# The end of a two-layer graph kernel: buffers of their own for the last normalisation, and another order of its loads and stores

## Chip, cores and metric

One NeuronCore of a Trainium2 chip runs the whole program. The metric is the device time of one execution in microseconds. One execution was recorded with the profiler; its times below count from the first instruction (the span's start).

## What is computed

x has 2048 rows of 512. A layer norm and a quantised graph layer give x1; then comes the layer that the end of the kernel works on:

```python
S = adj + I;  R = S / row_sums(S);  Xf = Xa = X = relu(layernorm(x1));  Z = 0
for s in range(2):
    A  = top_p_softmax(Xa @ W1 @ W2 @ (Xa @ W3).T)       # rows, P_TOP = 0.9
    Xf = R @ Xf
    Xa = A @ Xa
    Z  = Z + (Xf @ U1[s] + Xa @ U2[s])
Y = X + Z
out = x1 + (Y - mean(Y)) * rsqrt(var(Y) + 1e-5) * gamma + beta
```

## The kernel before

The 2048 rows are 16 tiles of 128 (T = 16), in four groups of four (G = 4, NG = 4). The second layer has two steps, s = 0 and 1. In step 1 each tile needs three things: its row of the diffusion R, added on GpSimd and written to the HBM tensor z1_d (`r_sum` line 651, `r_store` 396); its attention row, made on VectorE (`search`, `settle`), which leaves E's slot of the tile in two half-precision parts and signals `s_kept`; and the product of the attention row with the operand in VR.

**One tile on the way to the product.** `e_turned` (line 469) transposes the slot with four DMA transposes, one for each 512 columns, into the single buffer EC. Each waits until TensorE has used the same part for the tile before (`s_a`). `terms_product` (931) multiplies; 48 matmuls make a tile. ScalarE scales the result by `rden` (1260), which exists once VectorE has finished all four tiles of the group (1806). GpSimd adds the z that SyncE loaded from z1_d into ZT (`z_in` 429, sum in 698). ZT is one buffer, so `z_in(t)` waits for the sum of tile t - 1. Slots of E alternate: groups 0 and 2 use slots 0 to 3, groups 1 and 3 slots 4 to 7.

**The order around a group** is fixed by `step_order` (265): for each group `group_start`, which takes the rows of R that fall to it (one in group 0, four in groups 1, 2 and 3 of step 1), then `pairs` with its four tiles. All DMAs stand in SyncE's one queue, in program order; a wait there holds up everything behind it. A row of R needs three loads (`at_hi_in`, `at_lo_in`, `ad_in`, lines 384 to 394) and one store.

**The end.** Tiles 0 to 11 are normalised in three batches of four, tiles 12 to 15 one by one (`normed` 1833, `batch`, `end`, 1851 to 1867). VectorE takes batch 0, batch 1, tile 12, batch 2, tiles 13, 14, 15. The inverse root of each comes from GpSimd (`root` 682), whose order in the last group is: root of batch 0, sum of tile 12, roots of batch 1, tile 12 and batch 2, sum of tile 13, its root, sum and root of tile 14, of tile 15. A batch needs y from z1_d and x from x1_d, 1 MB each (`fin_in` 442), in E's slots 0 and 1 or 2 and 3: batch 2 uses the buffers of batch 0 and so waits for its store (`s_out`). All these loads are issued in `pairs` of the last group (491 to 498), ahead of the transposes of tile 13, and batch 2's at tile 13 (517). Tiles 12 to 15 lie in turn in UO and XF, so tile 14 waits for the store of tile 12 (1258); their x rows (`end_in` 457) go to WS, VectorE's scratch.

Of the kernel before, what the change touches and what calls it, by code (L numbers as in the profile page):

```python
# [8 lines left out]
P = 128  # L9
N, D, DA = 2048, 512, 64  # L10
T = N // P
KC = D // P
G = 4
# [85 lines left out]
def build(nc, x, adjT, scal, w, W1T, W2, W3, U10, U11, U20, U21, gamma, beta, out):  # L99
    ctx = ExitStack()  # L100
    with ctx:
# [79 lines left out]
        fin_y = [E[:, 2 * h, :].rearrange("p (t d) -> p t d", t=G) for h in range(2)]  # L181
        fin_x = [E[:, 2 * h + 1, :].rearrange("p (t d) -> p t d", t=G) for h in range(2)]
# [5 lines left out]
        gam, ends = WF, (UO, XF)  # L188
        end_x = WS[:, :].rearrange("p (t d) -> p t d", t=G)
# [59 lines left out]
        s_finx, s_finy, s_end = ([sem(f"{n}{h}") for h in range(2)] for n in ("s_finx", "s_finy", "s_end"))  # L249
        s_endx = sem("s_endx")  # L250
# [48 lines left out]
        def _(sp):  # L299
# [142 lines left out]
            def fin_in(b):  # L442

                rows = slice(G * b, G * b + G)
                if b >= 2:
                    sp.wait_ge(s_out, 16 * (b - 1))
                sp.dma_start(fin_x[b % 2], x1_d[rows].rearrange("t p d -> p t d")).then_inc(s_finx[b % 2], 16)
                sp.wait_ge(s_yout, 16 * (G * b + G) + OPEN)
                sp.dma_start(fin_y[b % 2], z1_d[rows].rearrange("t p d -> p t d")).then_inc(s_finy[b % 2], 16)

            def fin_out(b, nth):
                sp.wait_ge(s_res, nth)
                if b:
                    sp.wait_ge(s_out, 16 * b)
                sp.dma_start(out[G * b:G * b + G].rearrange("t p d -> p t d"), fin_y[b % 2]).then_inc(s_out, 16)

            def end_in():
                sp.wait_ge(s_kept, 2 * T)
                sp.dma_start(end_x, x1_d[T - G:T].rearrange("t p d -> p t d")).then_inc(s_endx, 16)

            def end_out(t, nth):
                sp.wait_ge(s_res, nth)
                sp.dma_start(out[t], ends[t % 2][:, :]).then_inc(s_end[t % 2], 16)
# [14 lines left out]
            def group_start(s, g):  # L478
                if s == 0 and g:
                    stores(G * g - 1)  # L480
                rows = diffusion(s, g)
                for rs, t in rows[:-1]:
                    r_done(rs, t, t % 2)
                for c in range(NC):
                    e_turned(g * G + s * T, g * G % (2 * G), c)
                for rs, t in rows[-1:]:
                    r_done(rs, t, t % 2)

            def pairs(s, g):
                last = s == 1 and g == NG - 1  # L490
                if last:
                    sp.wait_ge(s_wl, T)
                    sp.wait_ge(s_gb, 16)
                    sp.dma_start(gam[:, :], gamma.partition_broadcast(P)).then_inc(s_gb, 16)
                    for c in range(NC):
                        sp.wait_ge(s_et[c], 16 * (T + G * (NG - 1)))
                    fin_in(0)
                    fin_in(1)
                for i in range(G):
                    t = g * G + i  # L500
                    following = (t + 1 + s * T, (t + 1) % (2 * G))
                    if s:
                        z_in(t)
                    if i < G - 1:
                        for c in range(NC - 1):
                            e_turned(*following, c)
                    if s == 0 and i:
                        stores(t - 1)
                    if i < G - 1:
                        e_turned(*following, NC - 1)  # L510
                    if s and not last:
                        y_store(t)
                    if last and i == 0:
# [35 lines left out]
            end_out(T - G + 2, 6)  # L549
            end_out(T - G + 3, 7)  # L550
            sp.wait_ge(s_rout, 16 * T + OPEN)
            sp.wait_ge(s_out, 16 * BATCHES)
            for h in range(2):
                sp.wait_ge(s_end[h], 16 * (G // 2))
# [3 lines left out]
        def _(pool):  # L558
# [127 lines left out]
            def pairs(s, g):  # L686
                for i in range(G):
# [7 lines left out]
                    y = ends[t % 2] if g == NG - 1 else UO  # L695
# [350 lines left out]
        def _(act):  # L1046
# [200 lines left out]
            def a_out(s, g, t, slot, bank):  # L1247
# [72 lines left out]
        def _(dve):  # L1320
# [530 lines left out]
            def batch(b, nth):  # L1851
                dve.wait_ge(s_finx[b % 2], 16 * (b // 2) + 16)
                dve.wait_ge(s_finy[b % 2], 16 * (b // 2) + 16)
                normed([(G * b + t, fin_y[b % 2][:, t, :], fin_x[b % 2][:, t, :]) for t in range(G)], nth)

            def end(t, nth):
                dve.wait_ge(s_y, t + 1 + OPEN)
                normed([(t, ends[t % 2][:, :], end_x[:, t - (T - G), :])], nth)
# [37 lines left out]
```

## Time and profile before

| | |
|---|---|
| three runs, median (lowest to highest) | 1296.33 us (1292.09 to 1300.24) |
| profiled execution, its own time | 1295.24 us |
| its span | 1293.3 us |
| TensorE busy | 1119.5 us, 87% |
| VectorE busy | 1035.7 us, 80% |
| ScalarE, GpSimd busy | 439.4 us, 281.2 us |
| mean granted TensorE clock | 0.953 |
| moved by DMA | 170.62 MB, mean 132 GB/s |

The busy shares are averages over the whole span. The end has limits of its own: in the last 25 us of the trace TensorE, VectorE and the DMA engines all have holes, so the chain of waits and the timelines of that stretch say more than the table. A bracket at the end of a row of a timeline gives the idle time of that engine before it, and what ended it.

### The profile page before, as it was taken

What the parts mean: (1) busy time and instruction counts of PE and PEld (TensorE: products, weight loads), DVE (VectorE), ACT (ScalarE), POOL (GpSimd) and SP (SyncE); (2) the same over time, 40 slices, a digit from 0 to 9 for tenths busy, and PEclk for the clock granted to TensorE, in tenths of its full rate; (3) what the DMA queues carried; (4) which work ended last, traced back from release to release, by engine and by line L of the source; (5) the groups of instructions that cost most, each with busy time, mean ns of one, the idle gap of its engine ahead of it and who ended that gap; (6) DMA issues with size and microseconds to landing.
All of it is one profiled execution on the core that took longest, in us unless ns stands there. A gap on an engine that the chain in (4) does not pass through costs nothing.

```text
span 1293.3 us, 16644 instructions
## 1 busy us (share of the span) xinstructions
PE 1119.5 (87%) x5402; PEld 518.1 (40%) x5402; DVE 1035.7 (80%) x2202; ACT 439.4 (34%) x836; POOL 281.2 (22%) x252
## 2 busy tenths in 40 slices
PE   0567999998999799799997999898999799789764
PEld 0223445454434344344443444343444344334321
DVE  7987777773599998899698006998997999999965
ACT  2544344444633033533432237540241251100000
POOL 6133333333122200101112010421111021011012
PEclk9888999999999899899998999898999899899887
DMA  7126466453334542341732513236844552743595
GB/s 244 65 69 220 166 205 209 168 199 118 95 117 153 143 89 43 90 82 42 147 82 66 96 51 130 90 117 243 193 91 136 134 115 90 187 114 107 148 266 156
DMA packets 190115, 170.62 MB, mean 132 GB/s; under 512 B 144656, under 2 KB 144656, under 8 KB 185936
## 3 DMA queue, kind: packets, MB, share of 16 engines
q1 hardware_dynamic: 190032, 169.66, 46.7%
q8 instruction: 34, 0.56, 0.2%
q14 instruction: 49, 0.40, 0.1%
HBM read 87.31 MB, written 48.76 MB: 105 GB/s over the span
## 4 chain that ended last, share of the span: by engine, by line
DVE 34%; PE 27%; issue 20%; POOL 7%; DMA 5%; ACT 5%; SPq 1%; POOLq 1%; DVEq 1%; ACTq 0%
PE RB L937 5%; DVE WS L1490 5%; DVE cand L1708 4%; PE UB L775 4%; PE AB L937 4%; DVE E L1721 3%; PE XB L775 3%; DVE WS L1705 3%; DVE WS L1713 3%; PE RB L939 3%; DVE g L1570 2%; PE AB L939 2%; DMA AD<-xu_d 2%; DVE E L1461 2%; DVE E L1720 2%
## 5 line engine op out<-in xcount | busy, mean ns | idle before, releaser
L1570 DVE TENSOR_REDUCE g<-E 128x1 f32<-128x2048 f32 x32 | 73.0, 2281 | 100.3 <-ACT E L1160 100.0
L1490 DVE SCALAR_TENSOR_TENSOR WS<-E,g 128x2048 bf16<-128x2048 f32 x48 | 119.6, 2535 | 0.4
L655 POOL TENSOR_TENSOR RT<-RT,AD 128x512 f32<-128x512 f32 x32 | 56.5, 1765 | 289.3 <-ACT RT L1220 289.2
L1708 DVE MAX8 cand<-WS 128x8 f32<-128x128 f32 x512 | 102.1, 276 | 1.1
L937 PE MATMUL AB<-VR,turns 128*128 128x512 f16 x256 | 66.3, 406 | 27.7 <-DMA turns<-E 27.7
L1713 DVE SCALAR_TENSOR_TENSOR WS<-E,g 128x2048 f32<-128x2048 f32 x33 | 80.9, 2450 | 0.9
L937 PE MATMUL RB<-VR,turns 128*128 128x512 f16 x256 | 64.2, 396 | 19.5 <-DMA turns<-E 19.5
L1721 DVE SCALAR_TENSOR_TENSOR E<-WS,E 128x2048 f16<-128x2048 f32 x32 | 79.1, 2472 | 1.1
L937 PE MATMUL RB<-XR,turns 128*128 128x512 f16 x256 | 63.8, 394 | 17.9 <-DMA turns<-E 17.9
L1197 ACT ACTIVATE E<-E,nmx 128x2048 f32<-128x2048 f32 x32 | 63.7, 1993 | 42.9 <-DVE nmx L1571 42.9
L672 POOL TENSOR_TENSOR XHL<-WF,XHL 128x512 f16<-128x512 f32 x16 | 22.1, 1383 | 250.0 <-ACT XHL L1245 250.0
L1705 DVE SCALAR_TENSOR_TENSOR WS<-E,g 128x2048 f32<-128x2048 f32 x32 | 75.5, 2360 | 1.1
L758 PE MATMUL AB<-E,turns 128*128 128x512 f16 x256 | 61.6, 397 | 8.9 <-DVE E L1391 5.9
L937 PE MATMUL AB<-XR,turns 128*128 128x512 f16 x256 | 62.3, 387 | 8.0 <-DMA turns<-E 8.0
L1407 DVE TENSOR_REDUCE E<-E (+1 forms) x16 | 59.2, 3703 | 3.1 <-issue 2.6
L899 PE MATMUL AB<-VR,turns 128*128 128x512 f16 x256 | 61.5, 379 | 0.0
L765 PE MATMUL AB<-E,turns 128*128 128x512 f16 x256 | 61.3, 384 | 0.0
L899 PE MATMUL AB<-XR,turns 128*128 128x512 f16 x256 | 56.7, 379 | 2.8 <-POOL XR L618 2.8
L899 PE MATMUL RB<-VR,AH 128*128 128x512 f16 x256 | 56.9, 379 | 0.0
L698 POOL TENSOR_TENSOR UO<-UO,Khl 128x512 f32<-128x512 f32 x14 | 25.3, 1804 | 145.0 <-ACT UO L1260 140.8
L899 PE MATMUL RB<-XR,AH 128*128 128x512 f16 x256 | 56.6, 379 | 0.1
L1412 DVE SCALAR_TENSOR_TENSOR turns<-E,turns (+1 forms) x16 | 38.7, 2420 | 21.0 <-ACT turns L1071 21.0
(316 smaller groups left out, 2210.0 us busy)
## 6 DMA issues: line engine op xcount, KB each, us to landing
turns<-adj_parts SPq DMA_DIRECT2D x48, 512.0 KB, 3.8
E<-adjT SPq DMA_DIRECT2D x16, 1024.0 KB, 7.6
adj_parts<-turns SPq DMA_DIRECT2D x16, 1024.0 KB, 5.2
AH<-adj_parts SPq DMA_DIRECT2D x16, 512.0 KB, 4.1
z_d<-UO SPq DMA_DIRECT2D x28, 256.0 KB, 2.3
XR<-x SPq DMA_DIRECT2D x4, 1024.0 KB, 11.8
WS<-U SPq DMA_DIRECT2D x4, 1024.0 KB, 7.5
x_d<-WF SPq DMA_DIRECT2D x16, 256.0 KB, 2.0
```

Source lines behind the costliest of these rows:

```text
L758: mm(AB[:, :], turns[:, h, 0, j, :], sup[:, j, :], start=(j == 0), stop=False)
L775: i = mm(dst, a(k), b(k), start=(first and n == 0), stop=(last and n == 3 * KC - 1))
L899: i = mm(bank[:, :], at_hi[odd][:, j, :], vs[:, j, k % 2, :], start=(k == 0), stop=False)
L937: mm(bank[:, :], EC[:, c, 0, b, :], xs[:, c * KC + b, y_, :], start=(c + b + y_ == 0), stop=False)
L939: i = mm(bank[:, :], EC[:, c, 1, b, :], xs[:, c * KC + b, 0, :], start=False, stop=(c == NC - 1 and b == KC - 1))
L1197: a(E[:, slot, :], E[:, slot, :], ACT.Exp, bias=nmx[:, slot:slot + 1], accum_out=tot[:, slot:slot + 1]).then_inc(s_exp, 1)
L1490: return v.scalar_tensor_tensor(junk[t % 2], e, g4[:, k, t:t + 1], e, op, ALU.mult, accum_out=g4[:, F_, t:t + 1])
L1570: ct(v.tensor_reduce(row(A2)[:, t:t + 1], E[:, slot, :], AX.X, ALU.max))
L1705: ct(v.scalar_tensor_tensor(WS[:, :], E[:, slot, :], g4[:, U, t:t + 1], E[:, slot, :], ALU.is_lt, ALU.mult, accum_out=g4[:, F_, t:t + 1]))
L1708: i = v.max(cand[:, t, 8 * c:8 * c + 8], WS[:, c * PART:(c + 1) * PART])
L1713: return v.scalar_tensor_tensor(WS[:, :], E[:, slot, :], g4[:, k, t:t + 1], E[:, slot, :], ALU.is_ge, ALU.mult, accum_out=g4[:, DEN, t:t + 1])
L1721: v.scalar_tensor_tensor(lo, kept, SE, hi, ALU.mult, ALU.subtract).then_inc(s_kept, 1)
```

## The change

The three batches get buffers that nothing else uses at that time: y in slots 0, 1 and 2 of E, x in UW, UV (weights of step 0) and slot 3 of E. Tiles 12 to 15 get one buffer each (UO, XF, RT, AD), and their x rows lie in XR instead of WS. The loads of x for batches 0 and 1 and of gamma are issued at the start of group 2 of step 1; y of batches 0 and 1 and x of batch 2 at the start of group 3, y of batch 2 after the first row of R there. In the last group the load of z for tile t + 1 stands behind the transposes of tile t + 1, the load of the x rows for the end behind those of tile 13, and all stores of results stand behind the last transposes and the last load of z. GpSimd's and VectorE's orders are unchanged.

```diff
-        fin_y = [E[:, 2 * h, :].rearrange("p (t d) -> p t d", t=G) for h in range(2)]
-        fin_x = [E[:, 2 * h + 1, :].rearrange("p (t d) -> p t d", t=G) for h in range(2)]
+        fin_y = [E[:, b, :] for b in range(NG - 1)]
+        fin_x = [u[:, :, :, :].rearrange("p k h d -> p (k h d)").bitcast(F32) for u in (UW, UV)] + [E[:, NG - 1, :]]
+        fin_y, fin_x = ([u.rearrange("p (t d) -> p t d", t=G) for u in us] for us in (fin_y, fin_x))
+        end_x = XR[:, 0:G, :, :].rearrange("p t h d -> p t (h d)").bitcast(F32)
...
-        gam, ends = WF, (UO, XF)
-        end_x = WS[:, :].rearrange("p (t d) -> p t d", t=G)
+        gam, ends = WF, (UO, XF, RT, AD)
...
-            def fin_in(b):
-
-                rows = slice(G * b, G * b + G)
-                if b >= 2:
-                    sp.wait_ge(s_out, 16 * (b - 1))
-                sp.dma_start(fin_x[b % 2], x1_d[rows].rearrange("t p d -> p t d")).then_inc(s_finx[b % 2], 16)
+            def fin_x_in(b):
+                sp.dma_start(fin_x[b], x1_d[G * b:G * b + G].rearrange("t p d -> p t d")).then_inc(s_finx[b], 16)
+
+            def fin_y_in(b):
                 sp.wait_ge(s_yout, 16 * (G * b + G) + OPEN)
-                sp.dma_start(fin_y[b % 2], z1_d[rows].rearrange("t p d -> p t d")).then_inc(s_finy[b % 2], 16)
+                sp.dma_start(fin_y[b], z1_d[G * b:G * b + G].rearrange("t p d -> p t d")).then_inc(s_finy[b], 16)
...
             def group_start(s, g):
                 if s == 0 and g:
                     stores(G * g - 1)
+                if s == 1 and g == 2:
+                    sp.wait_ge(s_wl, T)
+                    fin_x_in(0)
+                    fin_x_in(1)
+                    sp.wait_ge(s_gb, 16)
+                    sp.dma_start(gam[:, :], gamma.partition_broadcast(P)).then_inc(s_gb, 16)
+                if s == 1 and g == NG - 1:
+                    for c in range(NC):
+                        sp.wait_ge(s_et[c], 16 * (T + G * (NG - 1)))
+                    fin_y_in(0)
+                    fin_y_in(1)
+                    fin_x_in(2)
                 rows = diffusion(s, g)
-                for rs, t in rows[:-1]:
+                for j, (rs, t) in enumerate(rows[:-1]):
                     r_done(rs, t, t % 2)
+                    if s == 1 and g == NG - 1 and j == 0:
+                        fin_y_in(2)
...
             def pairs(s, g):
                 last = s == 1 and g == NG - 1
-                if last:
-                    sp.wait_ge(s_wl, T)
-                    sp.wait_ge(s_gb, 16)
-                    sp.dma_start(gam[:, :], gamma.partition_broadcast(P)).then_inc(s_gb, 16)
-                    for c in range(NC):
-                        sp.wait_ge(s_et[c], 16 * (T + G * (NG - 1)))
-                    fin_in(0)
-                    fin_in(1)
                 for i in range(G):
...
-                    if s:
+                    if s and (i == 0 or not last):
                         z_in(t)
...
                     if last and i == 0:
+                        sp.wait_ge(s_r, 2 * T)
                         end_in()
-                        fin_out(0, 1)
-                    if last and i == 1:
-                        fin_in(2)
-                        fin_out(1, 2)
-                    if last and i == 2:
-                        end_out(T - G, 3)
-                        fin_out(2, 4)
-                    if last and i == 3:
-                        end_out(T - G + 1, 5)
+                    if last and i < G - 1:
+                        z_in(t + 1)
+                if last:
+                    fin_out(0, 1)
+                    fin_out(1, 2)
+                    end_out(T - G, 3)
+                    fin_out(2, 4)
+                    for k in range(1, G):
+                        end_out(T - G + k, 4 + k)
...
                     if t >= T - G + 2:
-                        act.wait_ge(s_end[t % 2], 16)
-                    y = ends[t % 2] if t >= T - G else UO
+                        act.wait_ge(s_rout, 16 * T + OPEN)
+                    y = ends[t % G] if t >= T - G else UO
```

## Rows read from the trace of the kernel before

**Rows 1.** Chain of waits, 1228 to 1294: start us, duration us, what.
```profile
1230.86 0.07 DVE rden L1806
...
1249.85 0.99 POOL rstd L684
...
1265.69 1.45 POOL rstd L684
1267.14 1.58 POOL XF L698
...
1269.17 3.46 DMA turns<-E
...
1272.77 3.57 PE RB L937 x8
...
1284.69 0.88 PE RB L939 x4
...
1289.98 0.75 DVE XF L1848
```

**Rows 2.** VectorE's timeline, the end: start us, duration us, instruction.
```profile
1230.97 2.47 DVE L1838 BATCH_NORM_STATS2 st<-E 128x6 f32<-128x512 f32 x4
...
1236.73 3.62 DVE L1848 SCALAR_TENSOR_TENSOR E<-E,rstd 128x512 f32<-128x512 f32 x4
...
1246.03 2.74 DVE L1848 SCALAR_TENSOR_TENSOR E<-E,rstd 128x512 f32<-128x512 f32 x4
...
1250.94 0.75 DVE L1848 SCALAR_TENSOR_TENSOR UO<-UO,rstd,WS 128x512 f32<-128x512 f32 x1 [0.51 <-POOL rstd L684]
1262.53 2.47 DVE L1838 BATCH_NORM_STATS2 st<-E 128x6 f32<-128x512 f32 x4 [10.83 <-DMA E<-z_d]
```

**Rows 3.** SyncE's queue, timeline: start us, time to issue us, what.
```profile
1069.93 0.34 SPq L436 DMA_DIRECT2D z_d<-UO  x1
...
1076.01 0.33 SPq L390 DMA_DIRECT2D turns<-adj_parts  x1
...
1168.66 0.34 SPq L436 DMA_DIRECT2D z_d<-UO  x1
...
1176.89 0.34 SPq L390 DMA_DIRECT2D turns<-adj_parts  x1
...
1226.52 12.29 SPq L474 DMA_TRANSPOSE turns<-E  x4
...
1242.72 10.57 SPq L474 DMA_TRANSPOSE turns<-E  x4
1253.35 0.57 SPq L447 DMA_DIRECT2D E<-x_d  x1
```

**Rows 4.** TensorE's timeline: rows of R, then tiles 12 and 13.
```profile
1082.72 3.62 PE L901 MATMUL RB<-XR,turns 128*128 128x512 f16 x16
...
1183.61 3.62 PE L901 MATMUL RB<-XR,turns 128*128 128x512 f16 x16
...
1204.33 3.62 PE L901 MATMUL RB<-XR,turns 128*128 128x512 f16 x16
1216.06 3.50 PE L937 MATMUL AB<-VR,turns 128*128 128x512 f16 x8 [8.11 <-DMA turns<-E]
...
1237.37 3.57 PE L937 MATMUL RB<-VR,turns 128*128 128x512 f16 x8 [9.18 <-DMA turns<-E]
```

**Rows 5.** GpSimd's timeline: the root of batch 0.
```profile
1234.13 1.45 POOL L684 TENSOR_TENSOR rstd<-rstd,powc 128x4 f32<-128x4 f32 x1 [23.62 <-DVE rstd L1841]
```

**Rows 6.** Two stretches of 2 us: busy times, granted clock, DMA share, GB/s.
```profile
1226.00:1228.00 2.00, 2.00 (x11) 0.78 (x8) 1.97 (x3) 0.00 (x0) 0.00 (x0) 1.00 1.05 402
...
1276.00:1278.00 2.00, 2.00 (x7) 0.73 (x6) 0.00 (x0) 0.69 (x1) 0.07 (x1) 0.66 1.02 382
```

**Rows 7.** Line 386, the row loads of R: issue to landing.
```profile
DMA to landing us min/median/max: 3.6/3.8/13.6
```

**Rows 8.** Line 455, the stores of batches: issue to landing.
```profile
DMA to landing us min/median/max: 4.5/9.7/10.4
```

More of the change, by code:

```diff
@@ L248, in build @@
             "s_zin", "s_y", "s_yout", "s_fvar", "s_frs", "s_res", "s_out")]
-        s_finx, s_finy, s_end = ([sem(f"{n}{h}") for h in range(2)] for n in ("s_finx", "s_finy", "s_end"))
-        s_endx = sem("s_endx")
+        s_finx, s_finy = ([sem(f"{n}{b}") for b in range(NG - 1)] for n in ("s_finx", "s_finy"))
+        s_endx, s_end = sem("s_endx"), sem("s_end")
         s_xin = [sem(f"s_xin{b}") for b in range(NG)]
@@ L440, in z0_store @@
                 sp.dma_start(z0_d[t], UO[:, :]).then_inc(s_uout, 16)
-            def fin_in(b):
-                rows = slice(G * b, G * b + G)
-                if b >= 2:
-                    sp.wait_ge(s_out, 16 * (b - 1))
-                sp.dma_start(fin_x[b % 2], x1_d[rows].rearrange("t p d -> p t d")).then_inc(s_finx[b % 2], 16)
+            def fin_x_in(b):
+                sp.dma_start(fin_x[b], x1_d[G * b:G * b + G].rearrange("t p d -> p t d")).then_inc(s_finx[b], 16)
+            def fin_y_in(b):
                 sp.wait_ge(s_yout, 16 * (G * b + G) + OPEN)
-                sp.dma_start(fin_y[b % 2], z1_d[rows].rearrange("t p d -> p t d")).then_inc(s_finy[b % 2], 16)
+                sp.dma_start(fin_y[b], z1_d[G * b:G * b + G].rearrange("t p d -> p t d")).then_inc(s_finy[b], 16)
             def fin_out(b, nth):
                 sp.wait_ge(s_res, nth)
-                if b:
-                    sp.wait_ge(s_out, 16 * b)
-                sp.dma_start(out[G * b:G * b + G].rearrange("t p d -> p t d"), fin_y[b % 2]).then_inc(s_out, 16)
+                sp.dma_start(out[G * b:G * b + G].rearrange("t p d -> p t d"), fin_y[b]).then_inc(s_out, 16)
             def end_in():
-                sp.wait_ge(s_kept, 2 * T)
                 sp.dma_start(end_x, x1_d[T - G:T].rearrange("t p d -> p t d")).then_inc(s_endx, 16)
@@ L462, in end_out @@
                 sp.wait_ge(s_res, nth)
-                sp.dma_start(out[t], ends[t % 2][:, :]).then_inc(s_end[t % 2], 16)
+                sp.dma_start(out[t], ends[t % G][:, :]).then_inc(s_end, 16)
             def stores(t):
@@ L548, in _ @@
             step_order(1, nothing, nothing, r_one, r_span, group_start, pairs, last_post)
-            end_out(T - G + 2, 6)
-            end_out(T - G + 3, 7)
             sp.wait_ge(s_rout, 16 * T + OPEN)
             sp.wait_ge(s_out, 16 * BATCHES)
-            for h in range(2):
-                sp.wait_ge(s_end[h], 16 * (G // 2))
+            sp.wait_ge(s_end, 16 * G)
         @block.gpsimd
@@ L694, in pairs @@
                         root(0, 0, G)
-                    y = ends[t % 2] if g == NG - 1 else UO
+                    y = ends[t % G] if g == NG - 1 else UO
                     pool.wait_ge(s_zin, 16 * t + 16)
@@ L1851, in batch @@
             def batch(b, nth):
-                dve.wait_ge(s_finx[b % 2], 16 * (b // 2) + 16)
-                dve.wait_ge(s_finy[b % 2], 16 * (b // 2) + 16)
-                normed([(G * b + t, fin_y[b % 2][:, t, :], fin_x[b % 2][:, t, :]) for t in range(G)], nth)
+                dve.wait_ge(s_finx[b], 16)
+                dve.wait_ge(s_finy[b], 16)
+                normed([(G * b + t, fin_y[b][:, t, :], fin_x[b][:, t, :]) for t in range(G)], nth)
             def end(t, nth):
                 dve.wait_ge(s_y, t + 1 + OPEN)
-                normed([(t, ends[t % 2][:, :], end_x[:, t - (T - G), :])], nth)
+                normed([(t, ends[t % G][:, :], end_x[:, t - (T - G), :])], nth)
             dve.wait_ge(s_gb, 32)
```

## Prediction

> **What bounds the kernel now.** I read the chain of waits first, for its last 65 us, then the timelines of VectorE, SyncE's DMA queue, TensorE and GpSimd over the same stretch, and last what the DMA engines moved.
>
> The chain [rows 1] shows the last group ending on VectorE at 1230.9, when the reciprocals of the denominators are ready, then two batches of normalisation, the normalisation of tile 12 (its root on GpSimd at 1249.85), a hole, a root on GpSimd at 1265.69, the sum of tile 13 until 1268.72, the transposes of tile 15 at 1269.17, its matmuls from 1272.77 to 1285.57, and 7.7 us of tail to the span's end at 1293.3. VectorE's timeline [rows 2] names the hole: after 1251.69 it is idle for 10.83 us until the load of z for batch 2 lands. The queue [rows 3] says why it is so late: the load of x for batch 2 is issued at 1253.35 because it stands behind the transposes of tile 14, whose four instructions take from 1242.72 to 1253.29, and those stand behind the loads of batches 0 and 1 (tile 13's four: 12.29 us), the load for the end and the first store. TensorE [rows 4] sits idle 9.18 us before tile 13 for the same reason, but that is not the loss: everything after 1230.9 waits for VectorE's batches, and GpSimd's fixed order ties TensorE to them. GpSimd takes root 3 (batch 2) before the sum of tile 13 (lines 696 to 704), SyncE's load of z for tile 14 waits for that sum, and the transposes of tile 15 stand behind that load.
>
> **The parts, costed.**
>
> *Batch 2's loads early.* Its own buffers free them of the first store; x is issued at 1169 to 1171 and z at about 1180, and both have 70 us to land. VectorE then goes on from tile 12 to batch 2 at 1251.7 instead of 1262.53: 10.8 us earlier. From there the order is as before: 6.19 us from the start of the batch to the sum of tile 13 (1262.53 to 1268.72), so the sum ends at 1257.9; 0.45 us of queue and 3.6 us until TensorE starts, 1261.9; 12.8 us of matmuls, 1274.7; 7.7 us of tail, 1282.5. The queue in front of these transposes is as empty as before, so their 3.46 us stand.
>
> *What could take over at that point.* TensorE: tile 12 starts at 1216.06 and needs at most tile 15's 12.8 us, 1228.9. Tile 13's transposes are now issued chunk by chunk from about 1220.4 behind only a 256 KB load, so they are there when tile 12 ends, and tile 13 needs at most 12.8 more, 1241.7. Tile 14's transposes wait for the load of z for tile 13, and so for the sum of tile 12. That sum still stands behind root 0, which starts at 1234.13 for 1.45 [rows 5]; with 1.6 for the sum it ends at 1237.2, the transposes give data at 1241.3, and tile 14 ends before 1241.7 + 12.8 = 1254.5. Tile 15's transposes want its chunks at 1258, so 3.5 us of cover remain. That is why removing the idle 9.18 us counts for nothing: TensorE only reaches the next wait earlier. The load for the end (1 MB into the x rows' buffer) is issued at about 1229.6 and needed at 1248.8, cover 19 us. Tile 13's value is needed by GpSimd at 1256, made by 1243.
>
> *The 2.25 MB moved to the start of group 2* (x of batches 0 and 1, gamma). They go out after the store at 1069.93, three more instructions of the queue, ahead of two row loads; the second, issued at 1076.01, is needed at 1082.72 [rows 3, 4]. At the 402 GB/s that the engines move in the busiest stretch [rows 6] 2.25 MB take 5.9 us; with some 2 us of landing they are through by 1078.5, and the row load lands by 1081.5. Cost nothing.
>
> *The 3 MB moved to the start of group 3* go out after 1168.66, then 1 MB more at 1180. 3 MB take 7.8 us at that rate, through by 1179; the half row issued at 1176.89 lands by 1182.5 and is needed at 1183.61. The margin is only a microsecond, so bound it: the longest landing of a row load in the trace is 13.6 us (behind the 4 MB load near 872) [rows 7], and with it the half comes at 1190.5, 6.9 us late. Behind this lies a wait of 8.11 us of TensorE between the last row (end 1207.95) and tile 12 [rows 4], as tile 12's transposes wait for VectorE, and SyncE does not reach them later. Zero to 6.9, both hidden; I take nothing. If that cover were gone, it would still not reach the end until tile 14 ends after 1258.
>
> *VectorE beside the early traffic.* No row shows it under just this traffic. One final pass of a batch took 3.62 us, another 2.74 [rows 2]: 0.9 us of irregularity. Lower bound: that extra goes, -0.9. Upper: each of the seven loads moved costs one such extra on VectorE, which is the chain until 1230.9: +6.3. I take 0, as the large loads of before ran beside the last passes of the group and the first batch began on time at 1230.97.
>
> *The stores moved to the end.* SyncE reaches them after the load of z for tile 15, which waits for the sum of tile 14: batch 2 done at 1251.7 + 9.4 (a batch's length, 1230.97 to 1240.35) = 1261.1, root of tile 13 done 2.1 later (as tile 12's, 1248.77 to 1250.84), sum 1.6, 1264.8. From 1265.3 on the queue gets 3.25 MB, then two tiles of 256 KB, and the last tile at 1293.3 - 10.8 - 2.5 = 1280.0. At 382 GB/s, the rate while the last batch's store and the transposes of tile 15 ran together [rows 6], 3.75 MB take 9.8 us, and with 2 us of landing they are gone at 1277.1, 3 us before the last store is issued. Bounds: 0, and 13 us from the rival below. I take 0. Extra buffers for tiles 14 and 15 take away a wait on the stores; it wasn't in the chain with the loads early, so 0.
>
> **Sum.** 1293.3 - 10.8 = 1282.5 for the span. The profiled execution took 1295.24 with that span, so 1284.4; it lies 1.1 below the median of the three runs, 1296.33, so against the median 1285.5. I take 1285.5, a gain of 0.83%. What a measurement of this kernel can tell from no change is about 1%, 13 us.
>
> **Rivals.** (a) *All of TensorE's idle time goes.* Tiles 13 and 15 both waited for transposes behind bulk traffic; without the order on GpSimd, tiles 12 to 15 would run in one piece: 1216.06 + 12.8 + 3 x 10.4 (48 matmuls at full clock, half of 1183.61 to 1204.33 [rows 4]) = 1260, and with the tail 1267.7: 1270.7 against the median. For it: the idle rows. Against: root 3 stands in front of the sum of tile 13 in both kernels. Chance 0.03.
>
> (b) *The early traffic costs VectorE* some 4 us or more, or row loads slip by more than their cover: 1289 to 1292. For it: the half row's margin of one microsecond. Against: VectorE is busy with data long in place, and 8.11 us of idle lie behind. Chance 0.12.
>
> (c) *Slower: the stores pile up behind each other at the end.* Before, a store of a batch landed after 9.7 us in the median and 10.4 at the longest [rows 8]. Taken one after another from 1265.3, three batches (31.2) and four tiles (2.6 each, as the last store from 1290.7) end at 1306.9: 13.6 us over the old span, 1309.9 against the median. It decides from the point where 3.75 MB need longer than 25 us (1265.3 to 1290.7), under 150 GB/s; between this and 295 GB/s (gone by 1280.0) it only eats the gain. For it: all 3 MB of results now go out after 1265, none before. Against: the 9.7 us were landings beside loads and transposes. By the Trainium skill ("DMA: Bandwidth & Descriptors", Queues, rings and completion order), each DMA engine consumes the descriptors of a queue in ring order, so a last small store would stand behind all earlier ones; here the transposes of tile 13 behind 4.25 MB of loads agree. By that rule the order alone is against this change, and the rate decides. Chance 0.03.
>
> (d) *Nothing comes of it*: another wait takes the place of the load (the sum of tile 13, the half clock after each hole) and the time stays within 4 us of before, 1292 to 1300. For it: the program has three queues in a fixed order, and I follow them on paper. Chance 0.07. The forecast itself has 0.75.
>
> **How the numbers follow.** Around the forecast: tile 15 in less than its 12.8 us (the clock was at half of 2.4 GHz for its first matmuls, 3.57 us for eight; a full-speed tile takes 10.4) could give 1 us, the irregularity of VectorE 1 either way, the median of runs 1.5 to 2. So 1281.5 to 1289.5 from the forecast; for 8 in 10 overall I go to 1281 to 1290.5, which takes in the half of (b). Faster by over 1% (under 1283.4): 0.15 from the forecast's lower edge and 0.03 from (a), 0.18. Slower by over 1%: 0.03 from (c), 0.01 from the rest, 0.04. Within 1%: 0.78.
>
> **What would show it.** In the profile after: no idle of VectorE between tile 12 and batch 2; root 3 on GpSimd near 1255; tile 13 on TensorE straight behind tile 12; TensorE idle some 2 us before tile 14 and 7 to 9 before tile 15, which starts near 1262; the last batch's store landed before 1280. Wrong would be: tile 12 starting later than 1216; the start of batch 0 later than 1231; the last 256 KB landing more than 3 us after its issue; or tile 15 starting before root 3 is done.

## The result, and the profile after

The changed kernel takes 1285.62 us in the median (1284.44 to 1286.39, four runs); the kernel before took 1295.95 in the same comparison (1292.09 to 1300.24). The ratio is 0.9919, its 95% interval 0.9895 to 0.9944: 10.3 us less. The interval is clear of 1, although the gain is smaller than the 1% that the prediction took for the least that a measurement can tell. The predicted time was 1285.5.

The profiled execution has a span of 1282.4 us against 1293.3. First the chain of waits, start us, duration us, what; it answers to [rows 1].

```profile
1230.64 0.06 DVE rden L1806
...
1249.78 0.99 POOL rstd L684
1250.76 3.90 issue
...
1254.70 1.45 POOL rstd L684
1256.15 1.58 POOL XF L698
...
1258.17 3.45 DMA turns<-E
...
1261.76 3.57 PE RB L937 x8
...
1273.85 0.88 PE RB L939 x4
...
1279.15 0.75 DVE AD L1848
```

The same chain as before, with the hole gone: from the root of tile 12 to root 3 it is now 4.92 us (1249.78 to 1254.70) where it was 15.84. Root 3 still comes ahead of tile 13's sum, and tile 15's transposes behind that.

VectorE's timeline (start us, duration us, instruction), against [rows 2]:

```profile
1230.75 2.47 DVE L1838 BATCH_NORM_STATS2 st<-E 128x6 f32<-128x512 f32 x4
...
1250.87 0.75 DVE L1848 SCALAR_TENSOR_TENSOR UO<-UO,rstd,XR 128x512 f32<-128x512 f32 x1 [0.51 <-POOL rstd L684]
1251.53 2.46 DVE L1838 BATCH_NORM_STATS2 st<-E 128x6 f32<-128x512 f32 x4
...
1276.88 0.69 DVE L1838 BATCH_NORM_STATS2 st<-AD 128x6 f32<-128x512 f32 x1 [9.04 <-POOL AD L698]
```

Batch 2 begins with no idle time in front of it. The 10.83 us of idle before the batch are gone, and the wait that ends last on VectorE is now the 9.04 us before tile 15, for TensorE's last product.

SyncE's queue, the last group (start us, time to issue us), against the last three of [rows 3]:

```profile
1220.20 9.00 SPq L470 DMA_TRANSPOSE turns<-E  x4
...
1236.98 0.33 SPq L433 DMA_DIRECT2D Khl<-z_d  x1
1237.40 5.39 SPq L470 DMA_TRANSPOSE turns<-E  x4
1257.74 0.34 SPq L433 DMA_DIRECT2D Khl<-z_d  x1
1258.17 5.37 SPq L470 DMA_TRANSPOSE turns<-E  x4
...
1264.76 0.97 SPq L452 DMA_DIRECT2D out<-E  x2
```

Tile 13's four transposes take 9.0 us instead of 12.29 because each now waits for TensorE to free its part, not for loads in front. Tile 14's go at full pace, 5.39 us for four where they took 10.57.

TensorE's timeline, against [rows 4], tiles 12 to 15; a bracket is idle time before:

```profile
1215.87 3.39 PE L937 MATMUL AB<-VR,turns 128*128 128x512 f16 x8 [8.12 <-DMA turns<-E]
...
1227.73 1.89 PE L937 MATMUL RB<-VR,turns 128*128 128x512 f16 x8
...
1241.46 1.89 PE L937 MATMUL AB<-VR,turns 128*128 128x512 f16 x8 [3.20 <-DMA turns<-E]
...
1261.76 3.57 PE L937 MATMUL RB<-VR,turns 128*128 128x512 f16 x8 [9.78 <-DMA turns<-E]
```

Tile 13 runs straight behind tile 12, 9.6 us earlier than before, and nothing comes of that: tile 15 starts 9.78 us after the end of tile 14. The 8.12 us before tile 12 stand as they did; the loads moved into groups 2 and 3 used none of it.

**A yardstick.** The stretch before the last normalisations is the same program in every kernel here except for the moved loads, and its end moves about: batch 0 starts between 1230.75 and 1235.63 in the fourteen profiles behind this document, in no order of the kernels. The two profiles above are the two earliest; the other twelve start at 1232.80 or later. The spans expected before the runs took the early start for fixed, so several were missed by this drift alone. What the change touches is the stretch from the start of batch 0 to the end of the span. I call it the end: 62.33 us before (1293.3 - 1230.97), 51.65 after (1282.4 - 1230.75), 10.7 less. It takes the drift of the rest out of a single profile. It isn't exact: batch 0's pass of line 1844 took 3.75 us in the changed kernel and 2.73 before, and such single passes come and go between profiles. Two kernels profiled twice differ by 0.21 and 0.07 us; I read nothing from differences under 1 us unless the rows of one engine account for them.

### The profile page after: what moved, and what is told of

The parts are those of the page before. It is cut to its first block, busy times and chain, and to the rows that moved or that the text cites. A ratio compares the mean times of both kernels' runs of the same rounds, so it can differ in the third digit from the quotient of the medians.

```text
span 1282.4 us, 16640 instructions
## 1 busy us (share of the span) xinstructions
PE 1115.2 (87%) x5402; PEld 517.5 (40%) x5402; DVE 1037.7 (81%) x2202; ACT 439.6 (34%) x836; POOL 282.5 (22%) x252
## 4 chain that ended last, share of the span: by engine, by line
DVE 35%; PE 27%; issue 19%; POOL 7%; ACT 5%; DMA 5%; SPq 2%; POOLq 1%; DVEq 1%; ACTq 0%
PE RB L937 5%; DVE WS L1490 5%; DVE cand L1708 4%; PE UB L775 4%; PE AB L937 4%; DVE E L1721 4%; PE XB L775 3%; DVE WS L1705 3%; DVE WS L1713 3%; PE RB L939 3%; DVE g L1570 2%; PE AB L939 2%; DMA AD<-xu_d 2%; DVE E L1461 2%; DVE E L1720 2%
## 6 DMA issues: line engine op xcount, KB each, us to landing
XR<-x SPq DMA_DIRECT2D x4, 1024.0 KB, 11.8
```

## The experiments

In short, with the end from one profile of each:

| kernel | the end, us | ratio to before (95%) |
|---|---|---|
| before | 62.33 | |
| before, own buffer for batch 2 | 61.9 | 1.0003 (0.9989 to 1.0017) |
| before, tile 13's sum first | 54.92 | 0.9945 (0.9932 to 0.9959) |
| before, own buffer and its place | 54.55 | 0.9942 (0.992 to 0.9963) |
| changed, all loads at the head of the last group | 52.4 | 0.9918 (0.9904 to 0.9931) |
| changed | 51.65, 51.44 | 0.9919 (0.9895 to 0.9944), 0.992 (0.9905 to 0.9934) |
| changed, batch 2's loads late | 51.35 | 0.9907 (0.9884 to 0.9931) |
| changed, 3 MB more traffic | 50.93, 51.0 | 0.995 (0.9931 to 0.9968), 0.993 (0.9915 to 0.9945) |
| changed, TensorE kept busy | 50.64 | 0.9919 (0.9904 to 0.9935) |
| changed, stores back | 49.4 | 0.9902 (0.9877 to 0.9928) |
| changed, tile 13's sum first | 47.57 | 0.9877 (0.986 to 0.9894) |
| changed, all sums first | 43.59 | 0.9864 (0.9848 to 0.9881) |

### Which part of the change gives the time

**Stores back.** Only the order of the last group in SyncE's queue:

```diff
                         end_in()
+                        fin_out(0, 1)
+                    if last and i == 1:
+                        fin_out(1, 2)
+                    if last and i == 2:
+                        end_out(T - G, 3)
+                        fin_out(2, 4)
+                    if last and i == 3:
+                        end_out(T - G + 1, 5)
                     if last and i < G - 1:
                         z_in(t + 1)
                 if last:
-                    fin_out(0, 1)
-                    fin_out(1, 2)
-                    end_out(T - G, 3)
-                    fin_out(2, 4)
-                    for k in range(1, G):
-                        end_out(T - G + k, 4 + k)
+                    end_out(T - G + 2, 6)
+                    end_out(T - G + 3, 7)
```

> The changed kernel, with the stores of results back in their old places among the transposes; early loads and all buffers stay. My theory: the gain is batch 2 starting on VectorE when tile 12 is done. The first store only delays tile 14 on TensorE, by some 6 to 9 us, and 7 to 9 us of cover stand there (tile 14 ended at 1251.98, its successor is wanted at 1258); so the span is 1282.4 to 1283.5 and the ratio to the kernel before 0.991 to 0.993. Rival 'the gain comes from transposes that no longer stand behind stores': 4 to 10 us are lost, span 1286 to 1292.

Measured: 1284.78 us, ratio 0.9902, a little better than expected; span 1284.4 with batch 0 starting at 1235.0, so its end is 49.4 us, 2.25 shorter than in the changed kernel. TensorE's timeline of tiles 14 and 15:

```profile
1251.36 3.57 PE L941 MATMUL AB<-VR,turns 128*128 128x512 f16 x8 [8.16 <-DMA turns<-E]
...
1266.11 1.89 PE L941 MATMUL RB<-VR,turns 128*128 128x512 f16 x8 [2.28 <-DMA turns<-E]
```

The first store does delay tile 14, to 16.4 us after batch 0's start from 10.7, and the cover (the time by which tile 14 is done too early) holds: tile 15 starts 31.1 us after batch 0, as in the changed kernel (31.0). What I had not written down is that it then runs faster. After 9.78 us of idle, tile 15's first eight matmuls took 3.57 us and the tile 12.97; after 2.28 us they took 1.89 and the tile 10.53. The windows say the same of two stretches of 3 us (start and end, length, then busy us and instructions of TensorE's matmuls, its weight loads, VectorE, ScalarE and GpSimd, then granted clock, DMA share and GB/s). The changed kernel, tile 15:

```profile
1262.00:1265.00 3.00, 3.00 (x8) 1.03 (x7) 2.48 (x4) 0.00 (x0) 2.22 (x2) 0.50 0.92 177
```

The kernel with the stores back, tile 15:

```profile
1266.00:1269.00 3.00, 2.89 (x14) 1.39 (x15) 2.45 (x4) 0.00 (x0) 2.22 (x2) 1.00 1.01 197
```

Half of full speed against full speed. So with the loads early the place of the stores gives nothing; if anything it costs, by the half clock at tile 15's start (2.25 us of the end; the two ratios, 0.9902 and 0.9919, have intervals that overlap). The rival, that the gain comes from transposes no longer behind stores, falls.

**Own buffer only.** The kernel before, with UW and UV as buffers of batch 2 and no wait for a store; its loads stay at tile 13 in the queue.

```diff
                 rows = slice(G * b, G * b + G)
-                if b >= 2:
-                    sp.wait_ge(s_out, 16 * (b - 1))
-                sp.dma_start(fin_x[b % 2], x1_d[rows].rearrange("t p d -> p t d")).then_inc(s_finx[b % 2], 16)
+                sp.dma_start(fin_x[b], x1_d[rows].rearrange("t p d -> p t d")).then_inc(s_finx[b], 16)
...
```

> The kernel before, where batch 2 alone has buffers of its own (UW, UV) and its loads don't wait for the store of batch 0; they stay where they were in the queue. My theory: nothing. The loads were issued at 1253.35 because they stood behind tile 14's transposes, and the store they waited for was done about 1250. Span 1292 to 1294.5, ratio 0.998 to 1.001, VectorE idle 10 to 11 us before batch 2. Rival 'the shared buffer was the bottleneck': span 1282 to 1285, ratio 0.992.

Measured: 1295.76 us, ratio 1.0003; the end 61.9 us. VectorE waits 10.48 us in the same place, and batch 2 starts 31.2 us after batch 0 (1232.80) where it started 31.6 us after it [rows 2]:

```profile
1264.02 2.47 DVE L1838 BATCH_NORM_STATS2 st<-UW 128x6 f32<-128x512 f32 x4 [10.48 <-DMA UW<-z_d]
```

By itself the buffer gives nothing.

**Own buffer and place.** The same, with batch 2's loads right behind those of batch 1, at the head of the last group:

```diff
                     fin_in(0)
                     fin_in(1)
+                    fin_in(2)
...
                         fin_out(0, 1)
                     if last and i == 1:
-                        fin_in(2)
                         fin_out(1, 2)
```

> As the one before, and batch 2's loads stand with those of batches 0 and 1 at the head of the last group, so 6 MB stand ahead of tile 13's transposes instead of 4. My theory: VectorE starts batch 2 at 1251.7 without idle, tile 13 starts on TensorE 3 to 5 us later than before (1240 to 1243), and TensorE then runs tiles 13 to 15 nearly in one piece: tile 15 starts at 1262 to 1264, full clock, ends 1274 to 1276; span 1282 to 1285, ratio 0.991 to 0.994. So nearly the whole gain without starting anything in groups 2 and 3. Rival 'the loads must be out of the last group': the 2 MB more in front cost what they bring, span 1288 to 1293.

Measured: 1290.48 us, ratio 0.9942; the end 54.55 us. The direction held, the size did not: about 4 us were missing, and the profile's span, 1288.5 us, lies in the range of the rival. TensorE's tiles 13, 14 and 15:

```profile
1245.71 3.57 PE L937 MATMUL RB<-VR,turns 128*128 128x512 f16 x8 [14.74 <-DMA turns<-E]
...
1259.90 1.89 PE L937 MATMUL AB<-VR,turns 128*128 128x512 f16 x8 [1.96 <-DMA turns<-E]
...
1270.26 1.89 PE L937 MATMUL RB<-VR,turns 128*128 128x512 f16 x8
```

VectorE at tile 12, and ScalarE at tile 14:

```profile
1254.06 0.69 DVE L1838 BATCH_NORM_STATS2 st<-UO 128x6 f32<-128x512 f32 x1 [2.69 <-DMA WS<-x_d]
```
```profile
1274.32 0.69 ACT L1260 ACTIVATE UO<-AB,rden 128x512 f32<-128x512 f32 x1 [15.65 <-DMA out<-UO]
```

2 MB more in front of them bring tile 13's transposes and the x rows of the end later: TensorE idles 14.74 us, and VectorE, rid of its 10.83 us, now waits 2.69 us at tile 12. Batch 2 starts 23.05 us after batch 0 (1257.00) and not 20.8 as in the changed kernel. The chain of waits now runs through TensorE alone: tile 13's first transpose (10.33 us to land, behind the loads), tile 13, tile 14's first transpose (9.52 us, behind the load of the x rows and the first store), tiles 14 and 15 without a pause. ScalarE's row shows a wait too: tile 14's product is done by 1270.4, and its result waits for its place in UO until 1274.32, when tile 12's store has landed. That isn't in the chain; tile 15 is multiplied meanwhile, until 1280.8.

**All loads at the head of the last group.** The changed kernel in all else (stores at the end, a buffer for each tile):

```diff
-                if s == 1 and g == 2:
...
-                    fin_x_in(2)
                 rows = diffusion(s, g)
...
+                if last:
...
+                    for b in range(NG - 1):
+                        fin_x_in(b)
+                        fin_y_in(b)
```

> The changed kernel with all seven loads taken out of groups 2 and 3 and put at the head of the last group, ahead of the load of z for tile 12 and of the transposes of tile 13: 6.25 MB there. Buffers and the place of the stores as in the changed kernel. Beside the run with batch 2's loads in front of the old order (end of 54.55 us from the start of batch 0) it says how much of that kernel's 2.9 us over the changed kernel is the loads' place. My theory: tile 13 starts on TensorE 9 to 10 us after batch 0's start instead of before it, the x rows for the end land 1 to 2 us late for tile 12, tile 15 starts right behind tile 14 at full clock; 52 to 53.5 us from batch 0 to the end, ratio 0.992 to 0.995. Rival 'the place is all': 54.5 us or more, ratio 0.995 or more. Rival 'the place is nothing': 51.4 to 51.7.

Measured: 1286.58 us, ratio 0.9918; the end 52.4 us, both as expected or slightly better, though tile 13 starts 11.7 us after batch 0 and not 9 to 10. VectorE at tile 12, and TensorE's tiles 13 and 15:

```profile
1251.94 0.69 DVE L1833 BATCH_NORM_STATS2 st<-UO 128x6 f32<-128x512 f32 x1 [1.65 <-DMA XR<-x_d]
```
```profile
1244.63 3.57 PE L932 MATMUL RB<-VR,turns 128*128 128x512 f16 x8 [14.68 <-DMA turns<-E]
...
1267.11 1.89 PE L932 MATMUL RB<-VR,turns 128*128 128x512 f16 x8
```

Against the changed kernel the end is 0.75 to 1 us longer, and the ratios show no difference. That is two effects against each other, as the times of tile 15 on TensorE show. The end is its start, counted from batch 0's, what it takes, and a tail:

| kernel | tile 15 starts after | takes | tail |
|---|---|---|---|
| before | 41.80 | 12.80 | 7.7 |
| changed | 31.01 | 12.97 | 7.7 |
| changed, stores back | 31.11 | 10.53 | 7.8 |
| changed, all loads at the head | 34.21 | 10.54 | 7.7 |
| before, own buffer and its place | 36.31 | 10.54 | 7.7 |

With the loads at the head TensorE, not VectorE, sets tile 15's start: from tile 13 on it never pauses and is still 3.2 us late. It gets 2.4 us back because a tile that follows the last one at once runs at full clock (10.54 us, not 12.97). The step from the own-buffer-and-place kernel, 2.1 us, is by the rows the first store: there it stands in front of tile 14's transposes and TensorE idles 1.96 us before that tile; here it doesn't. The tiles' own buffers have no part in it.

**Batch 2's loads late.** The changed kernel, with the loads of batch 2 alone moved behind tile 14's transposes, issued at 1245.33 and 1245.95:

```diff
+                    if last and i == 1:
+                        fin_x_in(2)
+                        fin_y_in(2)
```

> The changed kernel, with the two loads of batch 2 taken out of group 3 and put behind the transposes of tile 14 (before the load of z for that tile), where the kernel before had them. Now the queue reaches this place at about 1243 instead of 1253, 2 MB land by 1251 and VectorE wants them at 1251.5. My theory: span 1282.4 to 1283.5, ratio as the changed kernel, 0.991 to 0.993. Rival 'only the early issue counts': VectorE idles before batch 2 by 5 us or more, span 1287 or more.

Measured: 1285.45 us, ratio 0.9907; the end 51.35 us. VectorE goes from tile 12 to batch 2 without a pause, 20.8 us after batch 0:

```profile
1253.16 0.75 DVE L1848 SCALAR_TENSOR_TENSOR UO<-UO,rstd,XR 128x512 f32<-128x512 f32 x1 [0.51 <-POOL rstd L684]
1253.83 2.47 DVE L1838 BATCH_NORM_STATS2 st<-E 128x6 f32<-128x512 f32 x4
```

So it isn't how early the loads go that counts, but whether they land before VectorE is done with tile 12. With the other 4 MB out of its way, tile 14's last transpose is issued 10 us sooner, and loads behind it land in time: they go out 12.3 us after batch 0's start where they went 22.4 us after it [rows 2, 3]. VectorE's hole closes in all three places tried for batch 2's loads: in group 3, at the head of the last group, and here.

### What ties TensorE to VectorE

The prediction said that root 3 stands ahead of the sum of tile 13 on GpSimd and that this holds tile 15. Three kernels move only this.

**The kernel before, tile 13's sum first:**

```diff
+                    if g == NG - 1 and i == 1:
+                        root(1, G, 2 * G)
                     y = ends[t % 2] if g == NG - 1 else UO
...
                     q.tensor_tensor(y[:, :], y[:, :], ZT, ALU.add).then_inc(s_y, 1)
                     if g == NG - 1:
-                        if i == 0:
-                            root(1, G, 2 * G)
-                        root(2 + i + (i > 0), t, t + 1)
-                        if i == 0:
-                            root(3, 2 * G, 3 * G)
+                        if i == 1:
+                            root(2, T - G, T - G + 1)
+                            root(3, 2 * G, 3 * G)
+                        if i:
+                            root(3 + i, t, t + 1)
```

> The kernel before, and only GpSimd's order changed: the sum of tile 13 right after root 1. Loads, stores and buffers as before. It separates VectorE's hole from TensorE's tie to it. My theory: VectorE still idles 10 to 11 us before batch 2 (its load stands where it stood), but tile 15's transposes no longer wait for it; they go out at about 1255 behind 3 MB of loads and a store, TensorE starts tile 15 near 1266; tiles 13 to 15 on VectorE end at 1281 to 1285; ratio 0.993 to 0.997. Rival 'the hole on VectorE is all': ratio 0.999 to 1.001.

Measured: 1289.27 us, ratio 0.9945; the end 54.92 us, 7.4 less than before, with no load moved. VectorE still waits for batch 2 (7.57 us, and 2.77 for tile 12's root, which now stands behind the sum), but TensorE's pause before tile 15 shrinks from 10.34 to 4.63:

```profile
1264.25 2.47 DVE L1840 BATCH_NORM_STATS2 st<-E 128x6 f32<-128x512 f32 x4 [7.57 <-DMA E<-z_d]
```
```profile
1268.67 2.89 PE L939 MATMUL RB<-VR,turns 128*128 128x512 f16 x8 [4.63 <-DMA turns<-E]
```

One addition moved on GpSimd gives two thirds of what the whole change gives. Batch 2 starts nearly as late after batch 0 (30.6 us where it was 31.6); it is only that tile 15 doesn't hear of it. VectorE's wait no longer sets the end: the chain of waits now runs from tile 13's late transposes through SyncE's queue, where the loads of batch 2 stand, to tile 15's transposes (issued at 1257.89, the first landing 10.64 us later), and VectorE idles 3.49 us before its last tile.

**The changed kernel, tile 13's sum first** (the same edit):

> The changed kernel with GpSimd taking the sum of tile 13 right after root 1 instead of after root 3. My theory: GpSimd's order, not the transposes' place, ties TensorE to VectorE's batches. Then the sum ends at about 1246.5, tile 15's transposes go out at 1247, TensorE runs tile 15 right behind tile 14 at 1251.9 to 1262.3 without falling to half clock, and VectorE's chain (batch 2 until 1261, tiles 13 to 15) becomes the bound, with the stores that start only at 1265 (3.75 MB, until 1276 to 1277): span 1275 to 1278.5. Rival 'TensorE waits for the transposes themselves': tile 15 starts at 1262 as before, span 1282.

Measured: 1280.23 us, ratio 0.9877; the end 47.57 us. The profile's span, 1283.2, is over the expected 1278.5; batch 0 starts 4.9 us later in it than in the changed kernel's, the latest of all. TensorE has one pause left in tiles 13 to 15, and tile 15 follows tile 14 at once:

```profile
1245.84 1.89 PE L939 MATMUL AB<-VR,turns 128*128 128x512 f16 x8 [2.81 <-DMA turns<-E]
```

The chain of waits now ends through GpSimd: the load of z for tile 15 waits for the sum of tile 14, which stands behind tile 13's root, and its 3.09 us are in the chain.

**The changed kernel, all sums first**, those of tiles 14 and 15 ahead of the roots of tiles 13 and 14 as well (against the kernel just above):

```diff
-                        if i:
-                            root(3 + i, t, t + 1)
+                        if i >= 2:
+                            root(2 + i, t - 1, t)
+                        if i == 3:
+                            root(3 + i, t, t + 1)
```

> As the one before, and the sums of tiles 14 and 15 stand ahead of the roots of tiles 13 and 14 too. The sum of tile 14 ends about 1257.7, the load of z for tile 15 and with it all stores go out 7 us earlier, at 1258. My theory: VectorE runs batch 2 and tiles 13, 14, 15 in one piece until 1270 to 1271, the stores are through before, span 1272.5 to 1275, ratio to the kernel before 0.984 to 0.986. Rival 'the stores or TensorE are next': span as in the one before.

Measured: 1278.24 us (1277.42 to 1279.11), ratio 0.9864; the end 43.59 us. It beats both kernels: 18.4 us under the one before in the same comparison (1296.65), some 7 under the changed one. Ratio and span (1276.6) come out just above what was expected; the step from the kernel just above is 4.0 us of the end, while the intervals of the two ratios overlap. GpSimd's order in its trace, from tile 13's sum:

```profile
1247.04 1.59 POOL L700 TENSOR_TENSOR XF<-XF,Khl 128x512 f32<-128x512 f32 x1
...
1257.98 1.44 POOL L684 TENSOR_TENSOR rstd<-rstd,powc 128x4 f32<-128x4 f32 x1 [3.94 <-DVE rstd L1845]
1259.39 1.61 POOL L700 TENSOR_TENSOR RT<-RT,Khl 128x512 f32<-128x512 f32 x1
```

and VectorE's last tile, which had waited 9.04 us:

```profile
1271.04 0.69 DVE L1842 BATCH_NORM_STATS2 st<-AD 128x6 f32<-128x512 f32 x1
```

From batch 0 on VectorE stops only for roots, half a microsecond each: now it is the bound of the end, not TensorE.

### The cover of the early loads, and the clock

**More traffic.** At the start of group 3 three copies of 1 MB each within HBM stand behind the three loads, in front of the rows of R:

```diff
                     fin_x_in(2)
+                    for k in range(3):
+                        sp.dma_start(xu10_d[G * k:G * k + G], x1_d[G * k:G * k + G]).then_inc(s_extra, 16)
```

> The changed kernel with 3 MB more, copied from one HBM tensor to another that is no longer read, right behind the three loads at the start of group 3. It tests the cover under the moved loads, which I took for 7 to 8 us of TensorE's idle before tile 12 (8.12 us after). My theory: the half row wanted at 1183.4 comes 3 to 9 us late, TensorE's idle before tile 12 shrinks by as much, the transposes of tile 12 still start at 1212.5, and the span stays at 1282 to 1284.5. Rival (b), early traffic reaches the end: span longer by 3 us or more.

Measured: 1288.43 us, ratio 0.995. It ran again beside the changed kernel itself:

> The kernel with 3 MB more at the start of group 3, again, beside the changed kernel: its four runs had a median 2.8 us over the changed kernel's, while its profile has the end unchanged (50.93 us from the start of batch 0). My theory: no real difference, the part before batch 0 varies by some us from run to run in all kernels, so the medians here lie within 1.5 us. Rival (b): 2 us or more are lost, before batch 0, on VectorE.

Measured: 1286.61 us, ratio 0.993.

> The changed kernel once more, so that the three others here can be set against it on the same chip. Ratio to the kernel before 0.990 to 0.994; from the start of batch 0 on VectorE to the end of the span 51 to 52.5 us (51.65 in its first profile, 62.33 before the change).

Measured: 1286.64 us, ratio 0.992 (0.9905 to 0.9934). In the trace of the first of the three, the half row waits as the bound of the prediction wanted it to, and more:

```profile
1193.99 6.39 PE L905 MATMUL RB<-XR,turns 128*128 128x512 f16 x16 [9.06 <-DMA turns<-adj_parts]
...
1243.99 3.56 PE L941 MATMUL AB<-VR,turns 128*128 128x512 f16 x8 [2.16 <-DMA turns<-E]
```

9.06 us of idle (0.23 in the changed kernel's second profile, none in its first), and the rows of R end at 1221.1 where they ended at 1207.75, with batch 0 only 2.9 us later. The 8.12 us of idle before tile 12 are used up, and the end doesn't grow: 50.93 and 51.0 us against 51.65 and 51.44. The span, 1284.6, is 0.1 over what was expected and 2.2 over the changed kernel's, less than the 3 us of the rival and less than batch 0's drift. So the bound's 6.9 us would have been hidden, and there was cover beyond that: pauses of 2.16 us before tile 14 and 8.67 before tile 15 still stand.

What did move is VectorE in front of batch 0. From the reciprocals of group 2 to the start of batch 0 it takes 95.73 and 95.71 us in these two profiles and 94.0 to 95.1 in the twelve others (94.18 in the changed kernel, 94.23 before). That is 0.6 us above the highest of the others (95.13, in the kernel with TensorE kept busy, which has no extra traffic) for 3 MB, in two profiles that agree. In the rows it is not spread out: single instructions take 0.9 to 1 us longer than the same one in another profile (the pass that starts at 1213.58 took 3.24 us where it took 2.35 in the changed kernel), and which ones do varies in all kernels. The medians of the second comparison are the same, 1286.61 and 1286.64. Whether the traffic causes it stays open.

**TensorE kept busy.** 34 matmuls of 512 columns on data that no one uses, between tiles 14 and 15:

```diff
+                if qq == 2 * T - 1:
+                    pe.wait_ge(s_lc, 2 * T * NC + OPEN)
+                    for _ in range(34):
+                        mm(LB[0][:, :], ident[:, :], VR[:, 0, 0, :], start=True, stop=True)
```

> The changed kernel with 34 extra matmuls of 512 columns on TensorE between tiles 14 and 15, into a bank that nothing reads; they take 7.3 us of the 9.8 us that it idles there. They test what half the clock costs in the chain: tile 15 took 12.97 us after (1261.76 to 1274.73) and 10.4 in the run with the stores back, where only 2.3 us of idle preceded it. My theory: tile 15 takes 10.4 to 10.6 us, the stretch from batch 0 to the end is 49.0 to 49.8 us, 2.3 us shorter than the changed kernel's. Rival 'the slow start comes from the data, not from the idle time': no change, or longer where the extra matmuls are in the way.

Measured: 1285.57 us, ratio 0.9919; the end 50.64 us: 1.0 us shorter than the changed kernel's 51.65, 0.8 than its repeat's, where 1.8 at least were expected.

```profile
1254.98 7.50 PE L971 MATMUL LB<-VR,ident 128*128 128x512 f16 x34
1265.13 3.26 PE L937 MATMUL RB<-VR,turns 128*128 128x512 f16 x8 [2.65 <-DMA turns<-E]
```
```profile
1255.00:1262.00 7.00, 7.00 (x34) 3.18 (x33) 6.89 (x15) 0.69 (x1) 3.03 (x2) 1.00 0.00 0
1265.00:1268.00 3.00, 2.87 (x7) 1.04 (x8) 2.41 (x5) 0.00 (x0) 2.23 (x2) 0.51 1.02 195
```

The clock was full through the extra work and at half 2.65 us after it. Tile 15 took 11.9 us and not 12.97: 1.1 us, the size by which the end fell. A tile at full clock throughout (10.53) would have given 2.4. The rival that tile 15's data make the slow start falls elsewhere: the same eight matmuls took 1.89 us with the stores back and in the four kernels where tile 15 follows tile 14 at once. But the extra work did not keep the clock full over the last 2.65 us.

## Why the prediction was right

By its steps, in its order:

- *The hole goes, 10.8 us.* Right: batch 2 starts at 1251.53 (predicted 1251.7) and the end is 10.7 us shorter. What made VectorE's wait expensive was the tie to tile 15: with the tie alone removed, VectorE still idles 10.3 us in two parts, TensorE still 9.21 before tile 13, and 7.4 us of the end are gone. TensorE's 9.18 us [rows 4] were not the loss in the kernel before, but they stand right behind it: with the tie removed, or with all loads at the head, the chain of waits runs through tile 13's late transposes. That the kernel with all loads at the head comes within 0.75 us of the changed one is partly luck of the clock (3.2 us lost, 2.4 got back).
- *"Its own buffers free them of the first store."* True and worth nothing: alone 1.0003. The place in the queue gives the time. At the head of the last group it gives 0.9942 with the stores among the transposes and 0.9918 with the stores at the end, so the loads need not leave the last group; what TensorE loses there on tile 13 is mostly hidden by the full clock.
- *The order on GpSimd ties tile 15 to batch 2.* Right, and the most useful sentence: root 3 at 1254.70, sum of tile 13 until 1257.71 (1257.9), tile 15 at 1261.76 (1261.9). Rival (a) did not come, for the reason given. With that reason taken away TensorE's pause before tile 15 goes and 2.91 us before tile 14 stay; the time is 1278.24 us, not the 1270.7 that I had put to it, because VectorE becomes the bound first.
- *12.8 us of matmuls, 7.7 of tail.* 12.97 and 7.7. The half clock was in the row that I took the 12.8 from, so the sum held. What a full clock could give back I put at 1 us, and that was too small: in the stores-back kernel it gave 2.4 (12.97 to 10.53).
- *TensorE's side.* Tile 13 behind tile 12 and tile 14 at 1241.46 (1241.3), as said. The idle time before tile 14 was 3.20 us, not some 2, because tile 13 ran at full clock and ended at 1238.26.
- *Early loads, nothing.* Right: the second row's half had no wait, and 0.23 us in the kernel's second profile, so the margin of a microsecond was real. With 3 MB more it had 9.06 us, and that was hidden too: the upper bound of 6.9 us belonged to the cover, not to the range.
- *VectorE beside the traffic, 0.* Right for the change itself as far as one can tell (94.18 and 94.63 us against 94.23). Rival (b), 4 us or more, fell; whether twice the traffic costs some 1 us stays open.
- *Stores through by 1277.1, cost 0.* From 1268 to 1270 the engines moved 408 GB/s, from 1276 to 1278 68 GB/s. The stores of batches landed after 5.1 to 8.6 us, the last one by 1275.7, and the last tile's store, issued at 1279.93, landed 2.0 us later with nothing left in front of it. So rival (c) fell at its own point. (The sum's 9.8 us take a MB as a million bytes where the sums for the early loads take 1,048,576; with these it is 10.3 us and 1277.6, and nothing changes.) Putting the stores back gave no gain or loss that the ratios show.
- *Separate buffers for tiles 14 and 15, 0.* Not run alone, but the rows bear it out. Tile 14's result did wait for tile 12's store: until 1277.11 in the kernel before, 3.9 us in the own-buffer-and-place kernel. In both the chain of waits passes through tile 15 on TensorE and not through this. By the code, though, the stores can't go to the end without these buffers: tile 15's load of z waits for tile 14's sum, this for UO, and UO for a store behind that load.

The mechanism was right; how close the number came was luck. The forecast against the median rested on 1.1 us between one profiled execution and the median, and on batch 0 starting when it had: it started at 1230.75 against 1230.97, while the other twelve profiles drift up to 4.9 us later, and the profiled execution was again 1.2 us under its median.

## What to carry to other kernels

Find whose wait ends last, and then ask what the waiting instruction is queued behind: here a buffer's wait was drawn in the code, and the queue's order was the price. Then follow every engine with a fixed order for a step that makes one chain wait for another that it has no data from; here one addition moved ahead of roots on GpSimd was worth 7.4 us by itself, and three of them some 7 us more on top of the change. When two kernels come out equal, look whether the same wait sets the end in both: here a late TensorE at full clock nearly matched an early one at half. Compare short changes by the stretch that they touch, and the whole by ratios from the same chip.

## What the runs showed of the hardware

The clock after short idle times is not a matter of their length alone. After 1.75, 1.79, 1.96, 2.28, 2.37, 2.81, 2.91 and 3.20 us of idle, TensorE's next eight matmuls took 1.89 us, as in full-speed stretches (granted clock 1.00, 2.4 GHz); after 2.04, 2.16 and 2.65 us they took 3.26 to 3.56, as at half (0.50, 1.2 GHz). After 4.63 us they took 2.89, after 7.69 us and more 3.26 to 3.57. What decides in between no run here shows; tile 15 took 10.53 us from a full start, 11.9 to 12.97 from a half one.

DMA transposes behind loads: with 256 KB in front, tile 13's first data came as TensorE was ready for them; with 6.25 MB more in front, TensorE had them 11.7 to 11.8 us after batch 0's start and 14.7 us of idle. The Trainium skill ("DMA: Bandwidth & Descriptors", Queues, rings and completion order) says that a DMA engine takes a queue's descriptors in ring order, and these rows agree with it.
